# Where VectorE's side work stands beside a recurrent step: three blocks moved behind the new state

## What is computed

```python
def step(h, xs):
    xzt, xrt, xht = xs
    z = sigmoid(xzt + h @ U_z + vz)
    r = sigmoid(xrt + h @ U_r + vr)
    hh = tanh(xht + r * h @ U + vh)
    h_new = (1.0 - z) * h + z * hh
    return (h_new, h_new)
...
gate = einsum('bsd,ed->bse', x, Wg) + routing_bias      # top 4 of 8 experts, softmax
out = swiglu(x, Ws1, Ws2, Ws3)                          # the shared expert
eo = einsum('ebsh,edh->ebsd', sigmoid(h1) * h1 * h2, W3)
out = out + einsum('ebsd,bse->bsd', eo, weights)
```

## Time and profile before

| | us |
|---|---|
| median of 3 runs | 2702.14 |
| lowest and highest run | 2702.08, 2711.69 |
| span of the profiled execution | 2710.7 |
| TensorE busy | 2438.8 |
| VectorE busy | 1928.0 |
| ScalarE busy | 1156.0 |
| GpSimd busy | 397.4 |

### The profile page before, as it was taken

The page is one execution under the profiler, slowest core; times in us unless marked ns, Lnnn a source line. Parts: engine busy times, 40 slices in busy tenths (PEclk is TensorE's granted clock), DMA queues, the critical chain, the costliest instruction groups (busy, mean ns, idle before and its releaser), DMA issues. The chain is left out here.

```text
span 2710.7 us, 119359 instructions
## 1 busy us (share of the span) xinstructions
PE 2438.8 (90%) x50848; PEld 2039.3 (75%) x50848; DVE 1928.0 (71%) x7416; ACT 1156.0 (43%) x3693; POOL 397.4 (15%) x412
## 2 busy tenths in 40 slices
PE   3778999999999999987758869999999999999999
PEld 2555677777777777754536659999999999999998
DVE  4767777777777777788666766677767776677774
ACT  3225555555555555556436733333333333333333
POOL 0000000000000000000019702222222222222222
PEclk9678999999999999999868959999999999999999
DMA  6000000000000000010003240000000000000000
GB/s 185 2 2 3 5 5 5 6 5 5 5 5 6 5 5 5 11 38 27 4 32 106 76 114 7 9 9 9 9 9 9 9 9 9 9 9 9 5 5 6
DMA packets 53195, 53.68 MB, mean 20 GB/s; under 512 B 25126, under 2 KB 47288, under 8 KB 50746
## 3 DMA queue, kind: packets, MB, share of 16 engines
q1 hardware_dynamic: 47878, 30.57, 4.1%
q0 software_dynamic: 1728, 12.58, 1.4%
q10 hardware_dynamic: 3060, 2.90, 0.4%
HBM read 39.46 MB, written 6.57 MB: 17 GB/s over the span
## 5 line engine op out<-in xcount | busy, mean ns | idle before, releaser
L105 PE MATMUL p<-xn,m_h 128*128 128x128 f16 x6144 | 559.4, 220 | 0.0
L105 PE MATMUL p<-xn,m_l 128*128 128x128 f16 x3072 | 530.6, 220 | 0.0
L105 PEld LDWEIGHTS p<-xn,m_h 128*128 128x128 f16 x6144 | 481.2, 98 | 1.8
L607 PE MATMUL lg_b<-xn,lh 128*32 128x256 f16 x6144 | 302.2, 293 | 78.4 <-DVE lh L1089 70.5
L2141 POOL TENSOR_TENSOR xn<-qkv_w,xn 128x384 f16<-128x384 f32 x256 | 233.9, 914 | 898.3 <-ACT xn L2099 898.3
L1065 DVE STREAM_TRANSPOSE gt<-lg_b 128x512 f32<-128x512 f32 x324 | 230.1, 710 | 181.0 <-PE lg_b L607 180.6
L867 ACT ACTIVATE gl<-gt 128x128 f32<-128x128 f32 x324 | 100.2, 309 | 599.3 <-DVE gt L1065 598.6
L882 ACT ACTIVATE hm<-xy,b 128x512 f32<-128x512 f32 x512 | 347.9, 680 | 0.0
L105 PEld LDWEIGHTS p<-xn,m_l 128*128 128x128 f16 x3072 | 301.3, 98 | 0.7
L2025 PE MATMUL po<-m_h,xn 128*128 128x256 f16 x1536 | 293.3, 272 | 1.9 <-DVE xn L2180 1.9
L607 PEld LDWEIGHTS lg_b<-xn,lh 128*32 128x32 f16 x6144 | 160.6, 102 | 164.4 <-DVE lh L1089 120.1
(11 more groups left out here) (392 smaller groups left out, 6206.0 us busy)
## 6 DMA issues: line engine op xcount, KB each, us to landing
m_stage<-in_m_w POOLq DMA_DIRECT2D x12, 1024.0 KB, 5.4
hs<-in_m_w SPq DMA_DIRECT2D x16, 384.0 KB, 3.4
x_dram<-x SPq DMA_DIRECT2D x16, 128.0 KB, 2.1
xs<-in_l_wv SPq DMA_DIRECT2D x1, 2048.0 KB
attention_dram<-att SPq DMA_DIRECT2D x16, 128.0 KB, 3.0
xn<-x_dram SPq DMA_DIRECT2D x16, 128.0 KB, 2.5
xn<-attention_dram SPq DMA_DIRECT2D x128, 16.0 KB, 1.8
out_dram<-xn SPq DMA_DIRECT2D x16, 128.0 KB, 2.2
```

What stands on the lines that cost most here:

```text
L105: ins = pe.matmul(out, w[wp](k), x[xp](k), start=start, stop=last and k == KT - 1 and xp == 1, skip_group_check=True)
L607: last = pe.matmul(gate_block(ae, j, par), lh[:, part, ae, k, u, :], columns(w[name], k, j), start=False, stop=(part == 1 and k == KT - 1) ...
```

## The change

In slots 3, 6 and 8 VectorE's block `misc` moves from between zc and `new_state` to behind `new_state`. Slots 1 and 2 keep their place, and so does slot 0, whose block stands ahead of zc. In the other slots the call does nothing. In chunk 0, which has a block in slot 6 only, it now stands behind the first half of `m3_low` and the new state, and ahead of the second half.

```diff
                 if scans(i):
                     dve.scalar_tensor_tensor(out=zc[:, :], in0=zr[:, 0:16], scalar=1.0, in1=h32[:, :],
                                              op0=ALU.subtract, op1=ALU.mult).then_inc(z_parts, 1)
-                if slot != 0:
+                if slot in (1, 2):
                     misc(i, slot)
                 if i == 0:
                     m3_low(slot, 0)
                 if scans(i):
                     new_state(i, slot)
+                if slot > 2:
+                    misc(i, slot)
                 if i == 0:
                     m3_low(slot, 1)
```

## The result

The changed kernel took 2721.81 us (median of 4 runs, 2720.55 to 2727.81), the kernel before beside it 2705.50 (4 runs, 2702.08 to 2711.69): a ratio of 1.0055, 95% interval 1.003 to 1.0079. The forecast was 2710 us with a range up to 2717, so the time lies above the range. Twelve more executions of the changed kernel against 35 of the one before, in a later comparison, gave 1.003 (1.0011 to 1.0048), +8 us, which is the size of the forecast's difference.

What follows compares the result with a forecast made beforehand. TensorE's matmuls were taken to bound the last stage, with VectorE already last in slots 4, 7 and 9. 6.6 + 10.4 - 8.7 = +8.3 us on 2702.1 gave about 2710 us, range 2702 to 2717.

Steps and rivals of the forecast that it cites:

- the base: The unchanged kernel's median time, 2702.1 us, to which the forecast difference of +8.3 us was added.
- What bounds: Last stage: TensorE's matmul list sets a slot's length; VectorE already last by 0.07 to 0.20 us in slots 4, 7, 9.
- rival (a): Moved blocks are covered in slots 4 and 7, only gains count: -9 to -14 us, some 2690 us; chance 4%.
- Slot 3, 14 times: Output block behind the state delays slot 4's swiglu by 0.47 us, state no earlier: +6.6 us (4.8 to 7.0).
- Slot 6, 14 times: Next chunk's input block: state 0.38 us earlier, slot 7's swiglu net 0.74 later: +10.4 us (8.4 to 11.2).
- Slot 8, 15 times: Expert weights' low half: state 0.79 us earlier, slot 9's swiglu net 0.58 earlier: -8.7 us (-6.0 to -11.9).
- rival (d): Slot 8: wt_h comes over 0.10 us behind the new state, gain shrinks; sum +12.7 at half, +17 at none; 9%.
- The sum: Slots 3, 6 and 8 together: 6.6 + 10.4 - 8.7 = +8.3 us, ends +0.2 to +13.3.
- Chunk 0: Slot 6's block with no swiglu to push: state earlier, next reset product later; taken as 0 (-1.1 to +1.1 us).
- (b): Slots 4, 7, 9: rh_l ahead of GpSimd takes 0.17 us instead of 0.91: -13.4 us, 2689 us; chance 3%.
- (c): A wait of about 1.2 us in slot 7 lowers TensorE's clock: +36 us, 2738 us; chance 3%.

## Why the forecast was wrong, point by point

Two terms of the forecast were mis-sized. The larger is the base, 2702.1 us, put in with nothing for the scatter of executions: the four executions beside the changed kernel have a median of 2705.5, and 35 later ones 2711.6. The smaller is slot 3's 0.47 us per chunk, which measured 0.63. The path was right.

**What bounds.** Right, and it was what decided the sign. VectorE was the last in slots 4, 7 and 9, so blocks in front of their swiglu were paid. It was late there by only 0.07 to 0.20 us and busy 70% of the time, and that was enough; slot 3's block one slot further shows the reverse. One ground for it was misread: the waits for rh_l of 2.5 us, held against rival (a), all lie in slot 0. The distances from L1984 to L1989 carried the argument.

**Slot 3, 14 times.** The mis-sized term of the difference. Forecast 0.47 each and at most 0.50, +6.6 us; measured 0.63, +8.8 us in sum and in its own run's chunks (962.0 against 953.2). The step that failed here is the price of the wait for the block's own end. I took it from L1910, whose successor starts 0.44 behind it. But there a single wait stands between two instructions; here follow a wait, then a semaphore step, then the swiglu's own waits, and together they took 0.22 behind the end. The run without them gave 0.34, which had been the lower end of the term. By what the forecast quoted from the Trainium skill, "VectorE: DVE Perf Modes", section "The DRAIN you can't avoid", that a semaphore costs nothing extra, the term would have missed by more: 0.42. The same section adds that a next operation that is not held starts earlier, which is what zm, 0.34 us into L2229, shows; the forecast's "disagrees" left that out.

**Slot 6, 14 times.** Forecast 0.74, measured 0.73; three chunks, in which TensorE stood for the new state ahead of slot 7 before the change (chunks 3, 6 and 9, 0.71 us in all), pay 0.56. 11 x 0.73 + 3 x 0.56 = +9.7 us, forecast +10.4; its own run shows 961.8 against 953.2 for the 13 of them in chunks 2 to 14. Right. That slot 7's L1989 would lie over 1.3 us behind L1984 was wrong in form: 1.09, since rh_h came late as well and held L1984 too. That changes where TensorE waits, not how long.

**Slot 8, 15 times.** Forecast -0.58, measured -0.59, -8.9 us; 944.5 against 953.2 in its own run, for 14 of them. Right, and wt_h was there in time, so rival (d) falls.

**The sum.** With the measured steps 8.8 + 9.7 - 8.9 = +9.6 us against +8.3, and the profiles show +9.4 to +9.8 in chunks 2 to 15. Chunk 0, put at 0 with ends of 1.1, is 0.3 shorter in the first two profiles (47.6 against 47.9). Over many executions the ratio gives +8 (3 to 13), and the two medians lie 5.5 apart.

**The rivals.** (a), cover in slots 4 and 7: no, by the runs with one block each. (b), rh_l ahead of GpSimd: it stayed at 0.91 us in the changed kernel; a run that makes it true gave the gain that (b) describes and more. (c), the clock: 1.00 in the steady window, with waits of 0.7 us.

**The base and the range.** This is the larger miss. The range's upper end, 2717, was the sum's upper end, 2715.4, and 1.5 us. Nothing stood in it for the executions themselves, though the times before held a warning: 2711.69 beside 2702.08 and 2702.14. I took the low pair for the kernel's time and set the forecast on the median of the three; 35 executions have a median of 2711.6 and reach from 2700.6 to 2719.1. Six of the 35 are under 2703, and two of my three were: bad luck, as far as the runs tell. Two later comparisons gave medians of 2713.9 and 2713.2 for the unchanged kernel; whether the chip had a part in the low first times, no run shows. The forecast's difference added to a base of 2711.6 is 2720, and the first four runs of the changed kernel had 2721.8. The second cause, 2 us, is slot 3. That the long-run difference is near the forecast's is not luck: it is the three steps.

## What to carry to other kernels

Moving work off the path to one instruction puts it on the path to the next one: before such a move, look in the following step for how far its last arrival is from being waited for, and prefer a place where that is large (here slot 5, where rh_l is 1.1 us early, against slots 4, 7 and 9, where it is already late). Where an engine's small, urgent instruction meets a neighbour's long one, put it ahead of the unhurried work of its own list, and look whether that work is still unhurried there (zc in slot 7 was not). And set a forecast on the middle of many executions, with their spread in its range, not on the lowest of three.

## What the runs showed of the hardware

A wait for an instruction's own end, one semaphore step and the next instruction's waits took 0.22 us behind that end, and 0.30 more than letting the next instruction follow unawaited (0.64 against 0.34 behind its start). An instruction of 128x16 that takes 0.17 us took 0.91 (rh_l) or 0.76 to 0.79 (zc) when GpSimd's 128x384 difference was running. The steady part, 953 us with TensorE's clock at 1.00, repeats within 0.2 us, and what lies ahead of it scatters by some 11 us, most of it in a stretch with a granted clock of 0.79 to 0.84; that the clock is the cause is not shown. And TensorE shown as 98.7% busy still had 2.5% to give (a chunk of 68.43 down to 66.74 us).
